# Sampling attention with weighted tents made in turned layout for four batches at a time, and turned rows one group ahead in the 64-wide self attention

## The reference, cut to what matters

```
off  = (query @ w_off + b_off)            # 16 heads x 4 points x (x, y)
aw   = softmax(query @ w_attw + b_attw)   # 16 heads x 4 points
v    = value @ w_value + b_value          # 16 heads x 16 channels
ix   = place of the point, in rows;  hy = its height factor
w[q, h, row] = sum over the 4 points of  aw * hy * max(0, 1 - |ix - row|)      # a "tent"
out[q, h, :] = sum over rows of w[q, h, row] * v[row, h, :]
x = x + out @ w_out + b_out
```

## Time and profile before

| | us |
|---|---|
| median of three executions | 2930.9 |
| span of the profiled execution | 2934.9 |
| PE busy | 2558.6 (87%) |
| DVE busy | 1775.3 (60%) |
| ACT busy | 1337.9 (46%) |
| POOL busy | 809.9 (28%) |
| sampling attention, first to last instruction | about 236 |
| l2a, its loop | about 333 |
| mean granted TensorE clock | 0.934 |

### The profile page before, as it was taken

How to read it: one execution, slowest core, us unless ns; L and a number is a source line. 1 busy time by engine, 2 the same in 40 slices (tenths; PEclk the granted TensorE clock), 3 DMA queues, 4 the chain that set the end, 5 groups by cost and what they waited for, 6 DMA issues and landing times. The chain is left out here.

```text
span 2934.9 us, 48117 instructions
## 1 busy us (share of the span) xinstructions
PE 2558.6 (87%) x16117; PEld 1872.8 (64%) x16117; DVE 1775.3 (60%) x4091; ACT 1337.9 (46%) x3461; POOL 809.9 (28%) x627
## 2 busy tenths in 40 slices
PE   5998989999688779699998998977969888869997
PEld 2666756767455446467776776757955566449896
DVE  7876886588788634444444657873346588434443
ACT  2333654256777323434333445743432388324442
POOL 5533530054100134122211224641110044142222
PEclk8999999999877789799999999988989999889999
DMA  9001000000200423200001002042130300531110
GB/s 322 4 0 50 14 19 1 14 3 1 65 5 1 87 67 110 90 1 1 1 1 40 22 1 73 2 147 85 37 91 1 85 15 5 174 123 52 51 52 27
DMA packets 152052, 142.44 MB, mean 49 GB/s; under 512 B 59948, under 2 KB 136770, under 8 KB 151428
## 3 DMA queue, kind: packets, MB, share of 16 engines
q1 hardware_dynamic: 139668, 110.61, 12.9%
q0 software_dynamic: 10560, 27.19, 2.7%
q10 hardware_dynamic: 1584, 1.57, 0.2%
HBM read 98.14 MB, written 43.02 MB: 48 GB/s over the span
## 5 line engine op out<-in xcount | busy, mean ns | idle before, releaser
L962 POOL TENSOR_TENSOR room<-room 128x1024 f32<-128x1024 f32 x144 | 274.0, 1903 | 432.2 <-DVE room L895 431.9
L1435 PE MATMUL l3f_out<-room,Y 128*128 x624 | 141.1, 379 | 0.0
L889 DVE TENSOR_REDUCE room<-room 128x8 f32<-128x1024 f32 (+1 forms) x144 | 139.9, 971 | 0.7 <-ACT room L1038 0.7
L962 POOL TENSOR_TENSOR room<-room,Y 128x1024 f32<-128x1024 f32 x32 | 60.7, 1898 | 252.0 <-DVE Y L895 252.0
L1435 PEld LDWEIGHTS l3f_out<-room,Y 128*128 128x128 f32 x624 | 115.6, 190 | 14.1
L1036 ACT ACTIVATE room<-l2a_scores,Y 128x128 f32<-128x128 f32 x256 | 72.1, 381 | 86.6 <-DVE Y L881 86.6
L2478 POOL DMA_INDIRECT sorted_rows<-room,l1f_place_i x32 | 31.0, 968 | 279.7 <-DVE l1f_place_i L2189 270.8
L607 PE MATMUL l2a_proj<-room 128*128 128x256 f32 x384 | 97.5, 398 | 11.6 <-ACT room L986 11.6
L1036 ACT ACTIVATE room<-l1a_scores,room 128x128 f32<-128x128 f32 x256 | 71.6, 386 | 58.4 <-DVE room L881 58.4
L1036 ACT ACTIVATE room<-l0x_scores,room 128x128 f32<-128x128 f32 x256 | 70.7, 385 | 59.2 <-DVE room L881 59.2
L607 PEld LDWEIGHTS l2a_proj<-room 128*128 128x128 f32 x384 | 71.8, 196 | 24.7 <-issue 14.9
(11 more groups left out here) (842 smaller groups left out, 7084.3 us busy)
## 6 DMA issues: line engine op xcount, KB each, us to landing
sorted_rows<-head SPq DMA_DIRECT2D x1, 16640.0 KB, 57.2
room<-in_L_ffn_w SPq DMA_DIRECT2D x16, 1024.0 KB
room<-in_L_ffn_W SPq DMA_DIRECT2D x16, 1024.0 KB
Y<-sorted_rows SPq DMA_DIRECT2D x62, 130.0 KB
room<-in_ctx SPq DMA_DIRECT2D x24, 256.0 KB, 2.7
room<-sorted_rows SPq DMA_DIRECT2D x39, 130.0 KB
room<-results SPq DMA_DIRECT2D x8, 512.0 KB, 7.1
room<-in_L_ffn_routed_w SPq DMA_DIRECT2D x4, 512.0 KB
```

The source lines that it names most:

```text
L889: dve.tensor_reduce(rsum[:, u % 2, 0:SUMMED], p[:, u % (TURN + 1), 0:SUMMED, :], AX.X, ALU.add)
L962: pool.tensor_tensor(p[:, u % (TURN + 1), :, :], p[:, u % (TURN + 1), :, :], rinv[:, u % (TURN + 1), :].unsqueeze(2).to_broadcast([P, HEAD ...
L1435: mm = pe.matmul(obank[n % 2][:, 0:D], hT[:, n % 2, f, :], chip.room[:, bass.ds(at + (SLOT // 2 + f * D), D)], start=(f == 0), stop=(f == ...
```

## The change

Three edits.

1. **Sampling attention, rewritten.** The weights are made with the context rows on the partitions (turned layout), for the 512 queries of four batches at once. For each pair of points p of a unit (a unit k is a quarter of the heads' points of a group: 8 pairs; 16 units, 128 pairs in all) `distances` makes two lines in PSUM with one bf16 matmul each, 128 partitions x 512 columns: u = w(1 + ...) and v = w(1 - ...), the weighted rising and falling line of the tent (64 rows for each of two points). ACT takes Relu of u into `W`; DVE takes min(max(v, 0), W) in one instruction (`tent`). That is the finished weight, already turned: the Abs, the Relu on SBUF, the multiplication, the two additions, the transposes and the copies of `wT` are gone. `values` multiplies W with the values straight away, over 128 partitions, four 32-column matmuls for each batch, unit and half, and adds the four points of a head in PSUM. The edge row 63 is added by one f32 matmul of 512 columns for each half of the heads and group (`edges`), with small tiles e63 and eT prepared for it. Weight times place is split in three bf16 parts as before, and the weight too (`make_parts`, on DVE for group 0, on POOL later). POOL also normalises the rows, adds the output bias to x ahead of time and clears v. Two u banks and two v banks rotate: `distances` of pair n waits for `tent` of pair n - 2. One bank takes the look-ahead projections of the loop, each waiting for its predecessor to be emptied. w_value and w_out are loaded in permuted order with more, smaller DMAs.

2. **Ordinary attentions with 16-wide heads.** The zero matmul at L693 is gone; the first round of L698 starts the bank instead.

3. **l2a.** y of a group is turned one group earlier: it leaves section 0 and stands last in section 2 of the last task of the group before that one.

```diff
+    early = [] if small or ctxsrc else turns
+    body = [f for f in steady if f not in early]
...
             if g + 1 < PAIRS:
-                here.extend((g + 1, f) for n, f in enumerate(steady) if n * 3 * PER // len(steady) == r * 3 + sec and (f[0] != "y" or g + 1 >= first_turned))
+                here.extend((g + 1, f) for n, f in enumerate(body) if n * 3 * PER // len(body) == r * 3 + sec and turned_rows(g + 1, f))
+            if g + 2 < PAIRS and r == PER - 1 and sec == 2:
+                here.extend((g + 2, f) for f in early if turned_rows(g + 2, f))
...
                     if small:
-                        pe.matmul(out[:, 0:P], chip.zeros_b[:, :], chip.ident_b[:, :], start=True, stop=False, skip_group_check=True)
...
-                                               start=False, stop=(o == 1), skip_group_check=True)
+                                               start=(o == 0), stop=(o == 1), skip_group_check=True)
...
+        SLOT_OF = {(0, 1): ("c0", 1), (0, 4): ("c1", 1), (1, 0): ("x0", 1), (1, 3): ("v0", 1), (1, 7): ("v1", 1),
+                   (2, 4): ("s0", 1), (2, 5): ("s1", 1), (2, 6): ("s2", 1), (2, 7): ("s3", 1),
+                   (3, 0): ("e0", 1), (3, 2): ("w0", 1), (3, 3): ("y0", 2), (3, 4): ("y1", 2), (3, 5): ("q0", 2), (3, 7): ("q1", 2)}
+        OUT_AT = {(0, 3): 0, (0, 6): 1, (1, 1): 2, (1, 5): 3}
+        ADD_AT = {(0, 4): 0, (0, 7): 1, (1, 2): 2, (1, 6): 3}
...
+                def distances(k, p):
+                    n = k * PAIRS_U + p
...
+                    if n >= 2:
+                        pe.wait_ge(w_ready, n - 1)
+                    at = (p % 4 * 4 + p // 4 * 2) * NR
+                    pe.matmul(u_bank[n % 2][:, :], selector[0][0:KS, at:at + P], partsT[0:KS, k % 4, :], start=True, stop=True)
+                    pe.matmul(v_bank[n % 2][:, :], selector[1][0:KS, at:at + P], partsT[0:KS, k % 4, :], start=True, stop=True).then_inc(d_filled, 1)
...
+                    for e in range(4):
+                        at = o * D + (st * 4 + e) * 32
+                        mm = pe.matmul(o_bank[st][32 * e:32 * e + 32, j * P:(j + 1) * P], v[:, g % 2, j, at:at + 32], W[:, k % 2, tt * 4 + e, j * P:(j + 1) * P],
+                                       start=False, stop=(o == 1 and tt == 1), skip_group_check=True)
...
+                for k in range(-1, UNITS + 2):
+                    for i in range(PAIRS_U):
+                        if k + 1 < UNITS:
                             distances(k + 1, i)
+                        if 0 <= k < UNITS:
+                            values(k, i)
                         for x in tasks_at(k, i):
                             task(x)
+                        if k >= 4 and (k % 4, i) in OUT_AT:
+                            output((k // 4 - 1) * GR + OUT_AT[(k % 4, i)])
...
+                def tent(k, p):
+                    n = k * PAIRS_U + p
+                    dve.wait_ge(u_ready, n + 1)
+                    dve.scalar_tensor_tensor(out=W[:, k % 2, p, :], in0=v_bank[n % 2][:, :], scalar=0.0, in1=W[:, k % 2, p, :], op0=ALU.max, op1=ALU.min).then_inc(w_ready, 1)
...
+                def relu(k, p):
+                    n = k * PAIRS_U + p
+                    if p == 0 and k >= 2:
+                        act.wait_ge(sampled, k - 1)
+                    act.wait_ge(d_filled, n + 1)
+                    act.activation(W[:, k % 2, p, :], u_bank[n % 2][:, :], ACT.Relu).then_inc(u_ready, 1)
```

More of the change, by code:

```diff
@@ new lines, in deform_block, with tasks_at @@
+        OUT_AT = {(0, 3): 0, (0, 6): 1, (1, 1): 2, (1, 5): 3}
+        ADD_AT = {(0, 4): 0, (0, 7): 1, (1, 2): 2, (1, 6): 3}
+        BY_VECTOR = "qvw"
+        opening = [(0, x) for x in (() if first_turned else ("y0", "y1")) + ("q0", "q1", "c0", "c1", "x0", "v0", "v1")] + [(1, "y0"), (1, "y1")] + [(0, f"s{c}") for c in range(4)]
+        def tasks_at(k, i):
+            if (k % 4, i) not in SLOT_OF:
+                return []
+            name, ahead = SLOT_OF[(k % 4, i)]
+            x = (k // 4 + ahead, name)
+            return [x] if x[0] < NG and x not in opening else []
@@ L3400, in output @@
-                def output(n):
-                    pe.wait_ge(o_copied, n + 1)
-                    pe.matmul(o_bank[:, D:2 * D], chip.ones[0:1, 0:P], w.v["bo"][0:1, :], start=True, stop=False, skip_group_check=True)
-                    for c in range(KC):
-                        mm = pe.matmul(o_bank[:, D:2 * D], oT[:, c, :], w.v["o"][:, c, :], start=False, stop=(c == KC - 1), skip_group_check=True)
-                    mm.then_inc(y_filled, 1)
-                for x in ("y0", "y1", "q0", "q1", "c0", "c1", "s0"):
-                    if x[0] != "y" or not first_turned:
-                        task((0, x))
@@ new lines, in output @@
+                def output(b):
+                    pe.wait_ge(o_copied, 2 * (b // GR) + 2)
+                    if b:
+                        pe.wait_ge(y_added, b)
+                    else:
+                        wait_emptied(pe, last_opening[1])
+                    j = b % GR
+                    for c in range(2):
+                        mm = pe.matmul(y_bank[:, 0:D], oT[:, c, j * P:(j + 1) * P], w.v["o"][:, c, :], start=(c == 0), stop=(c == 1))
+                    mm.then_inc(y_filled, 1)
@@ L3500, in weigh_points @@
[L3500 to L3514 removed]
+                    dve.reciprocal(asum[:, :], asum[:, :]).then_inc(rinv_ready, 1)
@@ new lines, in _ @@
+                for x in opening:
+                    if x == (0, "v0"):
+                        exp(0)
+                    if x[1][0] not in BY_VECTOR:
+                        empty(x)
+                for k in range(-1, UNITS + 2):
+                    for i in range(PAIRS_U):
+                        if k + 1 < UNITS:
+                            relu(k + 1, i)
+                        if i == 0 and k >= 2 and k % 2 == 0:
+                            copy_out((k - 2) // 4, (k - 2) // 2 % 2)
+                        for x in tasks_at(k, i):
+                            if x[1][0] not in BY_VECTOR:
+                                empty(x)
+                        if k % 4 == 0 and i == 5 and k // 4 + 1 < NG:
+                            exp(k // 4 + 1)
+                        if k == UNITS - 2 and i == 7:
+                            act.preload_act_table(ACT.Sqrt)
+                        if k == UNITS - 1 and i == 2 and head:
+                            head.roots(act)
@@ L3693, in _ @@
                 if head:
-                    head.copy_second(act, dist[1][:, 0:512])
+                    head.copy_second(act, u_bank[1])
                 else:
```

670 lines of the change are left out of this document (345 added, 325 removed).

## The result

The changed kernel takes 2901.0 us (median of four executions, 2898.2 to 2903.9) against 2928.9 for the kernel before (four executions, 2926.5 to 2931.0): ratio 0.991, 95% interval 0.990 to 0.993, 28 us less. The spans of the profiled executions are 2896.5 and 2934.9, 38.4 apart. That of the kernel before is not one of the four timed ones: its span alone is longer than the longest of them.

A forecast was written before the change was run, and what follows sets the result against it. DVE and ACT were taken to bound the sampling block, PE to bound l2a and l1a. Gains of 24 + 12 + 7 = 43 off the profiled 2934.9 gave 2892, or 2888 as median; range 2860 to 2922.

The forecast's parts named there:

- The sum: Whole kernel: 24 + 12 + 7 = 43 us off the profiled 2934.9, giving 2892.
- l2a: 64-wide attention: turning rows a group early removes TensorE's wait for ACT's copy, 12 us, between 10 and 13.
- Sampling block, opening: Sampling block from its start to the first distances: 19.1 us, first distances at 782.2.
- the first eight DVE steps are as now, to 768.6: Sampling block's opening: VectorE's first eight steps keep their earlier times, ending at 768.6.
- Sampling block, loop: Sampling block's loop: 184 us, with 170 us of TensorE work at full clock and the rest stalls.
- The chain: Sampling block's loop: distances, Relu, tent and hand-overs take 2.0 us for two steps, against TensorE's 1.80 plus tasks.
- rival B: Sampling block: hand-overs add up, 15 us more in the steps and opening 5 longer, 2908; chance 0.20.
- Rival A: Sampling block and small attentions: mode changes are hidden, step 0.67, zero matmul brings 19, kernel 2861; chance 0.16.
- Tail: End of the sampling block: copy, four outputs with additions, statistics and barrier, 8.8 us.
- Rival C: Sampling block: TensorE's clock stays at 0.77, loop 235, kernel slower at 2939; chance 0.07.
- Zero matmul: Small attentions: leaving it out gains 0.055 us a task over 128 tasks, 7 us, between 5 and 19.
- 4.0 above the median: Whole kernel: profiled execution taken as 4.0 us above the median, turning 2892 into 2888.

The follow-up runs named there:

- pool_held: Changed kernel with one GpSimd wait for VectorE's first parts before the memset of v's second half; 2895.1 us, 2927.1 before in the same job.
- memsets: pool_held with six more GpSimd memsets of v's second half ahead of its wait; 2920.3 us in one execution, 2940.5 before in the same job.
- best1: pool_held plus edge-row projection one slot earlier, first v zeroing on ScalarE, selector columns earlier; 2898.8 us, 2940.5 before in the same job.
- few_values: Changed kernel with the values products left out in seven of eight steps of a unit; 2908.2 us in one execution, 2942.4 before in the same job.
- after_again: The changed kernel unaltered, run again in a later job; 2912.8 us, 2940.5 before in the same job.
- only_zero: Kernel before with only the zero matmul of the small attentions left out; 2922.7 us, 2927.1 before in the same job.
- only_sampling: Kernel before with only the new sampling block and its weights; 2922.6 us, 2927.1 before in the same job.
- only_l2a: Kernel before with only l2a's turned rows made a group early; 2908.3 us, 2927.1 before in the same job.

## Why the prediction was right or wrong

The sum said 43 and the change brings 28; the time, 2901.0, is 13 us above the forecast and inside its range, even inside 2874 to 2906, to which it gave 0.53. That is in part luck: two terms missed in opposite directions, the sampling block by 18.6 to the bad (24 said, 5.4 by block) and l2a by 7 to the good.

- **Sampling block, opening: wrong, and the largest miss.** 19.1 was said and 32.6 came. The step that failed is "the first eight DVE steps are as now, to 768.6": in the kernel before POOL is idle in this block, and the change gives it work there. The prediction counted that work (14 us a group) and called it hidden, asking only whether someone waits for its result, not whether it may run beside DVE. pool_held takes 10.9 us off by one wait, memsets puts 10.0 back by work that nobody needs. The 2.6 between pool_held's 21.7 and the 19.1 are not taken apart; best1, with its further edits to the opening, gets 18.8.
- **Sampling block, loop: right in size.** Said 184, measured 188.8 from the first distances to the copy of the last sums (793.93 to 982.72). The group with everything took 48.4 (said 49.5), the third 43.1 (44); a step 0.89 (0.90), the tent 684 ns (0.68), Relu 598 (0.59); y0 waits 1.95 behind L3610 (2.1), in two groups. Too low were the unit ahead, 12.8 for 9.5, the first group, 47.8 for 46.5, and the end, 36.7 for 34.5. The clock in the first 6 us of the unit ahead is 0.65, and the prediction reckoned the whole loop at full clock.
- **The chain: priced right, its nearness missed.** It was priced at 2.0 us for two steps, and few_values shows 2.01 where nothing lies between. What was missed is that TensorE's side work is mostly added to it: 1.36 a step over the loop, against the 1.4 that the loop takes. The mechanism of rival B, hand-overs that add up, is thus nearer than its chance of 0.20 said, and 2901 lies between the forecast and B's 2908; but the condition that was named for B, steps over 1.5 us with PE waiting for the tent at full clock, is met in single steps only: PE's waits for the tent are some 7 us in the loop. Anything that lightens PE alone brings little.
- **Rival A, the mode changes are hidden: false.** The step is 0.89 and not 0.67, and the 0.09 ahead of narrow matmuls stays (zero matmul, below).
- **Tail: right by its profile,** 9.0 for 8.8 from that copy on, but only at the higher clock; after_again took 12.8 with the same code.
- **Rival C, the clock stays low: false.** It is 0.98 over the loop and 1.00 from 852 on. The reason given against it, that the clock follows how full PE is, is no rule even in the rows at hand: the old sampling block has PE busy 79% at 0.77, l1f 73% at 0.85.
- **l2a: the mechanism right, the term mis-sized.** Said 12 (10 to 13), measured 18.8 alone. The six stalls are 12.7, the count of the earlier trace rows right. The missing 6.7 are four stretches at the lower clock behind four of the six stalls. The earlier trace rows counts only idle time; I did not compare the distances between groups, 47.1 and 45.4, which show the rest.
- **Zero matmul: right in sign and mechanism, somewhat too large.** 0.06 a task as said (L695 at 654.35 to L713 at 655.31, 0.96, for 1.02 in the earlier trace rows); the time is 4.4 for 7, below the lower bound of 5, with a 95% interval of 0.3 to 7. l1a as a whole gains nothing of its 32 x 0.06 (183.3 for 183.2), though PE gains 1.05 us on before from its fifth to its last task: ahead of the fifth task PE stands 2.58 for ACT in both, and behind it the scores take 1.03 and 2.08 at the lower clock in the changed kernel, 0.60 and 1.14 in before, 1.6 us in all. That clock is lower there in only_zero and only_sampling too and not in only_l2a, so it is no matter of this edit alone. Rival A's 19 from this edit is false: the 0.09 stays. That a change of tiling mode drains TensorE is what the Trainium skill states (TensorEngine Tiling (Array Packing), Key Properties); the trace agrees in that eight transposes (0.87) are followed by 0.09 without a zero matmul too, and no run here shows the drain itself.

```profile
654.35 1.04 PE L695 MATMUL l1a_probsT<-ident,room 128*128 128x128 f32 x8
655.31 0.65 PE L713 MATMUL l1a_out<-room 128*32 128x128 f32 x16
```

- **The sum against the profiled execution.** "4.0 above the median" was used as a constant and is none: the changed kernel's profiled span, 2896.5, is 4.5 below its median. The profile of before has the stand in l1f and the first of the changed kernel has not; the difference of the two, 38.4, is 10.9 too large for that reason, and 27.5 without it.

## What to carry to other kernels

When a change gives work to an idle GpSimd, look at what VectorE does in the same microseconds: here one-input operations on SBUF waited whole GpSimd instructions (0.29 to 1.96 us), and tents, with one input in PSUM, did not (0.68 with and without). So put the GpSimd work beside the latter. Price a stall of TensorE not by the idle time but by the distance from one group to the next, compared with a group without it. And when three engines hand pieces around a ring of two buffers, lay out the ring with all side work on its links: TensorE was 92% busy in this loop, and a second bound lay 5% behind it.

## What the runs showed of the hardware

- A VectorE tensor_scalar of 128 x 256 f32 on SBUF takes 0.29 us alone and 1.61 to 2.48 beside back-to-back GpSimd memsets of 1.91; a tensor_tensor with two SBUF inputs 0.42 alone, 0.40 beside memsets, 1.48 beside GpSimd additions (changed kernel, memsets, pool_held). The reduction L3557 took 0.40 to 0.41 in all three, and the tent with one input in PSUM 0.68 with GpSimd's 14 us beside the first unit of the loop (pool_held) and without.
- TensorE's lower clock (half of the higher) follows a stand of 1.93 to 2.04 us in some cases and not in others, in the same code: four of six in one execution of l2a, costing 1.68 us each, and 4.4 us at the end of l1x. After a stand of 2.58 us in l1a it is the lower one in the changed kernel and the higher one in before, 1.6 us.
- A stand of some 9 us in l1f, with inputs ready, is there in all four profiles of one job and in none of the four of another, on the same chip, with 4 to 5 us of lower clock behind it; the kernel before takes 2940 in the one and 2927 in the other. Comparisons of a few microseconds hold only within a job.
